# A last stage written anew: cosines spread by transfers, biases inside the turning products, all engines a batch apart

## The chip, the core and the metric

One core of a Trainium2 chip runs the whole kernel in one launch. PE (TensorE) multiplies matrices into PSUM, DVE (VectorE), ACT (ScalarE) and POOL (GpSimd) work on tiles of 128 partitions, SP issues most DMA transfers. Each engine takes its instructions in the order written; semaphores join them. The metric is the device time of an execution in microseconds (us).

## The reference, cut to what matters

A network of four layers runs on x of 8 x 512 x 128 floats; each adds `s * g` to x, where s is a sequence mixer and g a gate. The change lies in the last mixer, a state-space layer with rotated queries and keys (4 heads of 64, 128 states), on `u = layernorm(x)` seen as 8 batches of 512 tokens here:

```python
proj = u @ W_in                     # z 256, x 256, Bg 128, Cg 128, dt, A, trap 4 each, angles 32
theta = cumsum(angles * dt)         # per head, over the tokens
Bn, Cn = rmsnorm(Bg) * B_norm_w, rmsnorm(Cg) * C_norm_w
K = rope(Bn + B_bias, theta)        # x1*c - x2*s, x1*s + x2*c for the first 64 states, the rest as it is
Q = rope(Cn + C_bias, theta)
# chunks of 64 with a carried state in the reference; the kernel takes the equal form over all 512 tokens:
y = (Q K^T * decays * steps, lower triangle) @ x + D * x
s = (y * silu(z)) @ W_out;   x = x + s * silu(ffn)
```

## The kernel before, in words

`ssm_phase` (from L3364) is the last stage. It runs over 8 batches `i`, in each over 4 heads `h`, with data held as channels x tokens, 128 x 512 float32. PSUM has 8 banks of 512 columns: 0 to 2 for the products of queries and keys, 3 and 4 for projections and for spread cosines, 5 and 6 for the outputs, 7 for angles, gates and the result.

Per batch, PE projects keys and queries (`keys_and_queries`), the gates z, the means of the squares (`means`), the swapped projections (`turned`, with columns exchanged so that a rotation is a sum of two products), the angles and the tokens x (L3458). ACT makes gates (Silu), squares (L3550), roots as Ln and Exp (L3553, L3555), sine and cosine (L3558 to L3561), and the decays of a head (Exp, L3592 and L3594, seven instructions). A function set that ACT doesn't hold costs an ACT_TABLE_LOAD. DVE multiplies angles by steps (L3660), sums them over the tokens (scan, L3662), brings them into one turn (`one_turn`, five instructions, L3667 to L3678), and norms keys and queries (L3696, L3698).

Per head, cosine and sine rows (32 partitions) are spread to 128 partitions by matmuls with constant matrices (`spread`, L3473, four passes). ACT adds a head's bias to the normed keys and queries (L3569). DVE's `prepare` makes both products, each with one input in PSUM, then the smaller of two decays (`low`, L3728); POOL adds the products (L3613) to kq; PE multiplies keys by queries (L3484, eight passes); DVE's `weigh` multiplies by the decays (L3739, L3742, seven instructions), which POOL has multiplied by step factors on the diagonal blocks (L3637); PE multiplies by the tokens (L3496):

```python
v.scalar_tensor_tensor(out=t2[:, h % 2, n, :], in0=ps[:, 3, :], scalar=1.0, in1=tb[:, n, :],
                       op0=ALU.add, op1=ALU.mult)
last = v.scalar_tensor_tensor(out=t3[:, h % 2, n, :], in0=rot[:, n, :],
                              scalar=W("bc_rb")[:, n * H + h:n * H + h + 1], in1=ps[:, 4, :],
                              op0=ALU.add, op1=ALU.mult)
```

The order is written out by hand on each engine. PE: spread(0), the skipped part D x, spread(1), product(0), spread(2), product(1), spread(3), product(2), outputs of heads 0 and 1, angles of the next batch, product(3), the next batch's projections and means, outputs of heads 2 and 3, `turned`. POOL's step factors (`steps`, L3623 and L3629, three instructions a head) for all four heads stand at the start of the batch. SP (from L3385) sends the steps `dtb` (four transfers to 32 partitions, L3398), the summed decays `ellb` (four, to 128 partitions, L3403) and stores the result two batches later. After the last head DVE gates the outputs (L3761), PE projects them, DVE multiplies by the block's gate and adds (L3685, L3687).

Of the kernel before, what the change touches and what calls it, by code (L numbers as in the profile page):

```python
# [12 lines left out]
ALU = mybir.AluOpType  # L13
# [5 lines left out]
NB = T // 128  # L19
# [3344 lines left out]
def ssm_phase(nc, K, out_to):  # L3364
# [6 lines left out]
    Q_, K_ = 0, 1  # L3371
    with Stage(nc, K, at_once=True) as ctx:
        S = sems(nc, ctx, "ss", "dx bcps ang pj2 xt sq ms std rs norm at th n n1 c1 c2 clamp "
                 "sin abs cos cosm turn yz sps s gx sum stored z0 z0sb z1 z1sb")
        R = sems(nc, ctx, "ssr", "dt", 2)
        HD = sems(nc, ctx, "sh", "ell cps b0 t2 turned qk low dec m1 m2 dm a y", H)
# [3 lines left out]
        sq, xt, th = sb("sq", 2, T), sb("xt", NB, 256), sb("th", 3, T)  # L3380
        dtb, ellb, low = sb("dtb", 2, T), sb("ellb", H, T), sb("low", 2, NB, 128)
        tb, t2, t3 = sb("tb", 2, T), sb("t2", 2, 2, T), sb("t3", 2, 2, T)
        kq, dec = sb("kq", 2, 2, T), sb("dec", H, SPAN)
        mm, own = sb("mm", H, NB, 128), sb("own", NB, 128)
        y, table = sb("y", 2, T), sb("table", B)  # L3385
        block = stage_block(nc, K, ctx)

        @block.sync
        def _(sp):
            def store(i):  # L3390
                sp.wait_ge(S["sum"], i + 1)
                sp.dma_start(out_to[:, i * T:(i + 1) * T], X[:, i * T:(i + 1) * T]).then_inc(S["stored"], 16)

            for i in range(B):
# [5 lines left out]
                for h in range(H):  # L3400
                    sp.wait_ge(HD["dec"][h], i)
                    sp.wait_ge(HD["low"][h], i)
                    sp.dma_start(ellb[:, h, :], Rd[1, i * H + h:i * H + h + 1, :].to_broadcast([128, T])  # L3403
                                 ).then_inc(HD["ell"][h], 16)
                if i >= 2:
                    store(i - 2)
            store(B - 2)
            store(B - 1)
            sp.wait_ge(S["stored"], 16 * B)

        @block.tensor
        def _(pe):
            def project(i, bank, w):
                return pe.matmul(ps[:, bank, :], w, XN[:, i * T:(i + 1) * T], start=True, stop=True)  # L3414


            def keys_and_queries(i):
                pe.wait_ge(HD["t2"][H - 1], i)
# [3 lines left out]
            def means(i):  # L3422
                pe.wait_ge(HD["a"][H - 1], i)
                pe.wait_ge(S["sq"], i + 1)
                for n in range(2):
                    last = pe.matmul(ps[:, n, :], cst("mean"), sq[:, n, :], start=True, stop=True)  # L3426
                last.then_inc(S["ms"], 1)

            def turned(i):
                pe.wait_ge(S["std"], i + 1)  # L3430
                project(i, 0, W("in_turned")[:, 0:128])
                project(i, 1, W("in_turned")[:, 128:256]).then_inc(S["turn"], 1)

            def angles(i):
                if i >= 2:
                    pe.wait_ge(S["s"], i - 1)
                project(i, 7, W("in")[:, 768:896]).then_inc(S["ang"], 1)

            def gates(i):
                pe.wait_ge(S["at"], i + 1)  # L3440
                project(i, 7, W("in")[:, 0:128]).then_inc(S["z0"], 1)
                pe.wait_ge(S["z0sb"], i + 1)
                project(i, 7, W("in")[:, 128:256]).then_inc(S["z1"], 1)

            def out(i):

                pe.wait_ge(S["yz"], i + 1)
                pe.wait_ge(S["z1sb"], min(i + 2, B))
# [5 lines left out]
            def turn(i):  # L3454
                pe.wait_ge(S["yz"], i)
                pe.wait_ge(S["z1sb"], i + 1)
# [4 lines left out]
                last.then_inc(S["pj2"], 1)  # L3461
                if i:
                    out(i - 1)
                pe.wait_ge(S["norm"], i + 1)
                pe.wait_ge(S["cosm"], i + 1)
                pe.wait_ge(S["sin"], i + 1)

                def spread(h):

                    if h:  # L3470
                        pe.wait_ge(HD["t2"][h - 1], i + 1)
                    for n in range(2):
                        last = pe.matmul(ps[:, 3 + n, :], cst(("spread", "spread_sin")[n])[:, h * 128:(h + 1) * 128],  # L3473
                                         th[:, 1 + n, :],
                                         start=True, stop=True)
                    last.then_inc(HD["cps"][h], 1)

                def products(h):
                    pe.wait_ge(HD["turned"][h], i + 1)
                    if h:  # L3480
                        pe.wait_ge(HD["a"][h - 1], i + 1)
                    for jk in range(NB):
                        at, n = KEYS_AT[jk], T - 128 * jk
                        last = pe.matmul(ps[:, at // T, at % T:at % T + n], kq[:, h % 2, K_, jk * 128:(jk + 1) * 128],  # L3484
                                         kq[:, h % 2, Q_, jk * 128:T], start=True, stop=True)
                    last.then_inc(HD["qk"][h], 1)

                def outputs(pair):

                    for h in pair:  # L3490
                        pe.wait_ge(HD["a"][h], i + 1)
                    for jk in range(NB):
                        at, n = KEYS_AT[jk], T - 128 * jk
                        for h in pair:
                            r = slice(64 * (h % 2), 64 * (h % 2) + 64)
                            last = pe.matmul(ps[r, 5 + h // 2, jk * 128:T], xt[:, jk, h * 64:(h + 1) * 64],  # L3496
                                             dec[:, h, at:at + n], start=False,
                                             stop=(jk == NB - 1), skip_group_check=True)
                            if jk == NB - 1:
                                last.then_inc(HD["y"][h], 1)  # L3500

                spread(0)

                pe.wait_ge(S["xt"], i + 1)
                for n in range(2):
                    pe.matmul(ps[:, 5 + n, :], dx[:, n * 128:(n + 1) * 128], XN[:, i * T:(i + 1) * T],
                              start=True, stop=False, skip_group_check=True)
                spread(1)
                products(0)
# [5 lines left out]
                if i + 1 < B:  # L3515
                    angles(i + 1)
# [562 lines left out]
```

## Time and profile before

| | |
|---|---|
| median of 3 runs | 2919.72 us (2915.32 to 2923.3) |
| profiled execution, its own time | 2923.67 us |
| its span | 2921.9 us |
| PE, DVE, ACT, POOL busy in the span | 81%, 74%, 59%, 35% |
| mean granted clock of TensorE | 0.891 |
| the stage changed | 2579 to 2921.9 us |

Times in the trace are from the start of the span. The span leaves out a little of what the device time counts, here 1.8 us. The shares are means over stages with different limits, so the stage is read alone. In it PE issues a float32 matmul as two passes, each with a weight load.

### The profile page before, as it was taken

How to read it: one execution, taken by the hardware profiler on the slowest of the kernel's cores; microseconds unless marked ns; L12 is line 12 of the kernel's file. 1: busy time of each engine (PE TensorE's matmuls, PEld its weight loads, DVE VectorE, ACT ScalarE, POOL GpSimd, SP SyncE). 2: the span in 40 equal slices, each digit the busy share in tenths (PEclk: the TensorE clock that was granted, in tenths of full speed). 3: DMA queues.
4: the chain of work that ended last, by engine and by line, in shares of the span. 5: the costliest groups of instructions: out<-in, count | busy, mean ns of one | idle time of the engine just before them, and what ended most of it. 6: DMA issues, size and time to landing. Idle time of an engine off the chain costs nothing. (4 is left out here: it accounts for less than half of the span.)

```text
span 2921.9 us, 36852 instructions
## 1 busy us (share of the span) xinstructions
PE 2356.4 (81%) x10377; PEld 1044.9 (36%) x10472; DVE 2165.8 (74%) x5969; ACT 1709.4 (59%) x3093; POOL 1015.9 (35%) x979
## 2 busy tenths in 40 slices
PE   7666378786778999769999989778788888768887
PEld 2211267663343434333333333323331111234443
DVE  6999589995686665456666666587579999567777
ACT  4444344543656666462222278646579999677775
POOL 0222489992244555240000044200020000048886
PEclk8777566776889999889999999989889999889999
DMA  3112575625175765431111033100031111011110
GB/s 131 58 58 72 136 133 109 107 41 147 52 227 109 145 117 112 101 141 47 34 36 37 23 82 101 50 0 0 17 108 45 45 40 44 16 42 33 39 37 26
DMA packets 301385, 211.63 MB, mean 72 GB/s; under 512 B 157640, under 2 KB 266104, under 8 KB 300536
## 3 DMA queue, kind: packets, MB, share of 16 engines
q1 hardware_dynamic: 263216, 191.81, 24.5%
q0 software_dynamic: 19712, 14.96, 3.8%
q10 hardware_dynamic: 18256, 2.52, 0.5%
q8 instruction: 85, 1.39, 0.2%
q14 instruction: 116, 0.95, 0.1%
HBM read 136.18 MB, written 62.52 MB: 68 GB/s over the span
## 5 line engine op out<-in xcount | busy, mean ns | idle before, releaser
L3169 ACT ACTIVATE ca_pw<-ca_ps,ca_mx 128x512 f32<-128x512 f32 x512 | 342.7, 931 | 7.3 <-DVE ca_mx L3205 7.3
L3205 DVE TENSOR_REDUCE ca_mx<-ca_ps 128x1 f32<-128x512 f32 x512 | 311.2, 674 | 1.0 <-PE ca_ps L3136 1.0
L3002 DVE CUSTOM_DVE_ANT_0 mx_sums<-mx_ps,w_w2f 128x384 f32<-128x384 f32 (+3 forms) x512 | 218.1, 486 | 112.2 <-PE mx_ps L2957 110.7
L2945 PE MATMUL gm_ps<-gm_h,w_w2f 128*128 128x512 f32 x512 | 239.0, 607 | 3.1 <-DVE gm_h L3030 3.1
L3169 ACT ACTIVATION_READ_ACCUMULATOR ca_pw<-ca_ps,ca_mx 128x1 f32 x512 | 230.6, 450 | 0.0
L3136 PE MATMUL ca_ps<-qs,ks 128*128 128x512 bf16 x484 | 173.6, 399 | 59.2 <-ACT ca_pw L3169 39.5
L2644 ACT ACTIVATE ta_pw<-ta_ps,w_cst 128x1280 f32<-128x1280 f32 x128 | 168.0, 1322 | 35.8 <-PE ta_ps L2524 35.7
L3074 ACT ACTIVATE gm_h<-gm_ps,w_w2f 128x512 f32<-128x512 f32 x64 | 44.0, 687 | 218.4 <-PE gm_ps L2945 218.4
L2370 ACT ACTIVATE at_pw<-at_ps 128x1280 f32<-128x1280 f32 x128 | 157.1, 1238 | 23.7 <-PE at_ps L2337 23.6
L2776 DVE TENSOR_TENSOR ta_pw<-ta_pw,w_cst 128x384 f32<-128x384 f32 x128 | 70.7, 552 | 130.8 <-ACT ta_pw L2644 127.0
L2689 POOL DMA_INDIRECT Acc<-XN,f_idx x64 | 104.4, 1631 | 152.4 <-DVE XN L2747 137.8
L3146 PE MATMUL ca_o<-ca_pw,ca_vs 128*32 128x512 f32 x1024 | 138.4, 616 | 2.5 <-POOL ca_vs L3180 2.5
L2384 POOL MEMSET at_qs<- 128x1024 uint32 x4 | 3.7, 952 | 379.2 <-POOLq L2854 379.2
L3180 POOL TENSOR_TENSOR ca_vs<-VA,ca_rz 128x64 f32<-128x64 f32 x64 | 19.0, 297 | 329.3 <-DVE ca_rz L3192 329.3
L3136 PEld LDWEIGHTS ca_ps<-qs,ks 128*128 128x128 bf16 x512 | 40.2, 96 | 259.8 <-ACT ca_pw L3169 225.2
L724 DVE TENSOR_REDUCE rs_st<-rs_run 128x32 f32<-128x128 f32 x512 | 122.0, 284 | 13.4 <-ACT XN L749 13.2
L2945 PEld LDWEIGHTS gm_ps<-gm_h,w_w2f 128*128 128x128 f32 x512 | 91.3, 189 | 106.8 <-issue 101.5
L2401 DVE TENSOR_TENSOR at_pw<-at_pw,w_cb_f 128x384 f32<-128x384 f32 x128 | 70.4, 555 | 59.5 <-ACT at_pw L2370 59.5
L622 PE MATMUL ex_hps<-ex_xgt,ex_w 128*128 128x128 f32 x384 | 68.5, 333 | 48.1 <-ACT ex_h L778 25.3
L707 DVE TENSOR_TENSOR rs_run<-rs_st,rs_lay 128x96 f32<-128x96 f32 x512 | 105.6, 248 | 0.1
L2393 POOL TENSOR_SCALAR_AFFINE_SELECT at_pw<-at_pw 128x128 f32<-128x128 f32 x128 | 73.5, 575 | 91.0 <-ACT at_pw L2370 91.0
L2351 PE MATMUL at_o<-at_pw,at_va 128*32 128x256 f32 (+2 forms) x1280 | 95.8, 392 | 8.4 <-DVE at_pw L2401 5.9
(573 smaller groups left out, 6183.9 us busy)
## 6 DMA issues: line engine op xcount, KB each, us to landing
Pd<-s_p SPq DMA_DIRECT2D x48, 384.0 KB, 4.5
ex_w<-e_w SPq DMA_DIRECT2D x48, 256.0 KB
Qd<-rp_q SPq DMA_DIRECT2D x4, 2048.0 KB, 9.6
ss_ellb<-Rd SPq DMA_DIRECT2D x32, 256.0 KB, 3.3
qs<-Pd SPq DMA_DIRECT2D x32, 192.0 KB, 4.1
ks<-Pd SPq DMA_DIRECT2D x32, 192.0 KB, 4.2
Pd<-cs_p SPq DMA_DIRECT2D x16, 384.0 KB, 2.4
GX<-Qd SPq DMA_DIRECT2D x44, 128.0 KB
```

What stands on the lines that cost most here:

```text
L707: v.tensor_tensor(rows(n, 0, 3, half)[:, :, :, :, 0], state(n - 1, half).unsqueeze(1).to_broadcast([128, 3, V4, N]), given(n, KK, 3), ALU. ...
L724: v.tensor_reduce(state(n, half).rearrange("p v k -> p (v k)"), rows(n, 2, 2, half).rearrange("p r v k s -> p (v k) r s"), AX.XY, ALU.add) ...
L2351: last = pe.matmul(O[32 * a:32 * a + 32, G % 2, t0:t1], va[:, jk, G % GROUPS * GH + a].rearrange("p d x -> p (d x)"), pw[:, (GH * G + a) % ...
L2370: act.activation(pw[:, s % BUF, 0:SPAN], ps[:, s % 2, 0:SPAN], ACT.Exp, scale=float(1 / np.sqrt(D))).then_inc(S["power"], 1)
L2644: act.activation(pw[:, s % BUF, 0:SPAN], ps[:, s % 2, 0:SPAN], ACT.Square, scale=0.25 * 0.5 ** 0.5, bias=cst("rhalf")).then_inc(S["power"], 1)
L2689: g.indirect_dma_start(Acc, bass.IndirectOffsetOnAxis(ap=idx[:, u // 2, at:at + 1], axis=0), y[:, u % 2, c, :], None, compute_op=ALU.add). ...
L2945: last = pe.matmul(at, W(("h1", "h2")[layer])[:, j * 512 + f * 128:j * 512 + (f + 1) * 128], (h0, h1)[layer][:, j, :], start=(j == 0), sto ...
L3002: return v.tensor_tensor_reduce(out=sums[:, bank, at:at + n], in0=ps[:, bank, at:at + n], in1=K["w2f"]("down")[:, T - n:T], scale=-1.0, sc ...
L3136: pe.matmul(ps[:, q % BANKS, :], ks[:, G % 2, h % GH, jk * 128:(jk + 1) * 128], qs[:, G % 2, h % GH, :], start=True, stop=True).then_inc(S ...
L3146: last = pe.matmul(O[32 * a:32 * a + M, G % 2, :], vs[:, h % BUF, jk, :], pw[:, h % BUF, jk, :], start=(jk == 0), stop=(jk == NB - 1), ski ...
L3169: act.activation(pw[:, h % BUF, jk, :], ps[:, (h * NB + jk) % BANKS, :], ACT.Exp, bias=mx[:, h % H, jk:jk + 1], accum_out=z[:, h % H, jk:j ...
L3205: v.tensor_reduce(mx[:, h % H, jk:jk + 1], ps[:, q % BANKS, :], AX.X, ALU.max, negate=True).then_inc(S["top"], 1)
```

## The change

`ssm_phase` is rewritten; the arithmetic is the same.

- **Cosines.** `spread` and its constants go. ACT writes three rows of results, cosine, sine and minus sine, to `trig`. SP copies them for each head from SBUF to SBUF into `cs`, in two transfers: to partitions 0 to 31 cosine and minus sine, to 32 to 63 cosine and sine. Partitions 64 to 127 hold 1 and 0, set once. `cs` has two places (h even, odd); `trig` has one, and ACT waits with the next batch's until all four heads' copies have landed.
- **Biases.** ACT's biased copies go. DVE adds the head's bias inside both products, and both now have two inputs in SBUF; the first is written to kq itself, POOL adds the second to it.
- **Order.** Each engine's order spans two batches: DVE prepares head 0 of batch i+1 before it weighs head 3 of batch i, POOL makes step factors a batch ahead between the heads, ACT makes the next batch's sines at the start of a batch and its roots at the end. The two means share bank 7 one after the other, the two gates are one ACT instruction over banks 3 and 4.

The core of the diff (steps, `weigh`, `lowest`, `finish`, `store` and the angles keep their instructions):

```diff
+            def turns_of(i, h):
+                sp.wait_ge(S["cos"], i + 1)
+                if h >= 2:
+                    sp.wait_ge(HD["t2"][h - 2], i + 1)
+                else:
+                    sp.wait_ge(HD["t2"][h + 2], i)
+                at = slice(32 * h, 32 * h + 32)
+                sp.dma_start(cs[0:32, h % 2], trig[at, COS:DOWN + 1]).then_inc(HD["cs"][h], 16)
+                sp.dma_start(cs[32:64, h % 2], trig[at, COS:UP + 1:UP]).then_inc(HD["cs"][h], 16)
...
+            for i in range(B):
+                turns_of(i, 2)
+                if i + 2 < B:
+                    steps_of(i + 2)
+                if i + 1 < B:
+                    sums_of(i + 1, 0)
+                    sums_of(i + 1, 1)
+                turns_of(i, 3)
+                if i + 1 < B:
+                    turns_of(i + 1, 0)
+                    sums_of(i + 1, 2)
+                    sums_of(i + 1, 3)
+                    turns_of(i + 1, 1)
+                if i:
+                    store(i - 1)
...
+            def means(i, n):
+                if n:
+                    pe.wait_ge(S["ln0"], i + 1)
+                else:
+                    pe.wait_ge(S["sq"], i + 1)
+                    pe.wait_ge(S["at"], max(i + 1, 2))
...
+            for i in range(B):
+                products(i, 0)
+                if i:
+                    outputs(i - 1, (2, 3))
+                    if i + 1 < B:
+                        keys_and_queries(i + 1)
+                products(i, 1)
+                tokens(i)
+                if i + 1 < B:
+                    means(i + 1, 0)
+                products(i, 2)
+                if i + 1 < B:
+                    means(i + 1, 1)
+                skipped(i)
+                outputs(i, (0, 1))
                 if i:
                     out(i - 1)
...
+                products(i, 3)
                 if i + 1 < B:
                     turned(i + 1)
+                if i + 2 < B:
+                    angles(i + 2)
+                if i + 1 < B:
+                    gates(i + 1)
...
+            def turns(i):
+                act.wait_ge(S["clamp"], i + 1)
+                for h in range(H):
+                    act.wait_ge(HD["cs"][h], 32 * i)
+                act.activation(trig[:, UP, :], phase[:, i % 2, :], ACT.Sin)
+                act.activation(trig[:, DOWN, :], phase[:, i % 2, :], ACT.Sin, scale=-1.0)
+                act.activation(trig[:, COS, :], phase[:, i % 2, :], ACT.Abs).then_inc(S["abs"], 1)
+                act.wait_ge(S["abs"], i + 1)
+                act.activation(trig[:, COS, :], trig[:, COS, :], ACT.Sin, scale=-1.0, bias=cst("halfpi")).then_inc(S["cos"], 1)
...
+            for i in range(B):
+                if i:
+                    gates(i)
                 if i + 1 < B:
+                    turns(i + 1)
+                decays(i, 2)
+                if i + 1 < B:
+                    squares(i + 1)
+                decays(i, 3)
+                tokens(i)
+                if i + 1 < B:
+                    roots(i + 1)
+                    decays(i + 1, 0)
+                    decays(i + 1, 1)
...
+            for i in range(B):
+                more = i + 1 < B
+                turned(i, 1)
+                if more:
+                    steps(i + 1, 0)
+                turned(i, 2)
+                weighed(i, 2)
+                if more:
+                    steps(i + 1, 1)
+                turned(i, 3)
+                weighed(i, 3)
+                if more:
+                    steps(i + 1, 2)
+                    turned(i + 1, 0)
+                    weighed(i + 1, 0)
+                    steps(i + 1, 3)
+                    weighed(i + 1, 1)
...
+            def prepare(i, h):
+                v.wait_ge(HD["cs"][h], 32 * (i + 1))
+                v.wait_ge(S["bc"], i + 1)
+                v.wait_ge(S["rot"], i + 1)
+                for n, side_of in ((0, K_), (1, Q_)):
+                    v.scalar_tensor_tensor(out=kq[:, h % 2, side_of, :], in0=bc[:, n, :],
+                                           scalar=W("bc_b")[:, n * H + h:n * H + h + 1], in1=cs[:, h % 2, 0, :],
+                                           op0=ALU.add, op1=ALU.mult)
+                    last = v.scalar_tensor_tensor(out=side[:, h % 2, side_of, :], in0=rot[:, n, :],
+                                                  scalar=W("bc_rb")[:, n * H + h:n * H + h + 1], in1=cs[:, h % 2, 1, :],
+                                                  op0=ALU.add, op1=ALU.mult)
+                last.then_inc(HD["t2"][h], 1)
...
             for i in range(B):
+                more = i + 1 < B
+                prepare(i, 1)
+                lowest(i, 2)
+                weigh(i, 0)
+                if i:
+                    gated(i - 1)
+                prepare(i, 2)
+                lowest(i, 3)
+                weigh(i, 1)
+                prepare(i, 3)
+                weigh(i, 2)
+                if more:
+                    normed(i + 1)
                 if i:
                     finish(i - 1)
...
+                if more:
+                    turned(i + 1)
+                if i + 2 < B:
+                    add_angles(i + 2)
+                if more:
+                    lowest(i + 1, 0)
+                    lowest(i + 1, 1)
+                    prepare(i + 1, 0)
+                weigh(i, 3)
+                if i + 2 < B:
+                    one_turn(i + 2)
```

The loops over `i` are, in this order, SP's, PE's, ACT's, POOL's and DVE's.

## Rows read from the trace of the kernel before

**Rows 1.** Busy time by stretch: us; PE, PEld, DVE, ACT, POOL busy; PEclk, DMA share, GB/s

```profile
2740.80:2781.40 40.60, 35.19 (x117) 16.48 (x118) 31.96 (x64) 29.22 (x52) 33.05 (x37) 1.00 0.14 39
```

**Rows 2.** The chain that ended last, in time: start us, us, what

```profile
2602.17 0.67 DVE ss_t L3718
...
2819.49 2.42 PE ss_ps L3484 x8
...
2827.44 2.59 PE ss_ps L3414 x6
...
2841.66 1.97 PE ss_ps L3473 x4
...
2860.03 2.42 PE ss_ps L3484 x8
```

**Rows 3.** Waits of three batches, 2740.8 to 2862.5: us in total, times, longest

```profile
DVE ss_y L3761 <- PE ss_ps L3496: 10.9, 3, 3.6
```

**Rows 4.** DVE in order of time, first stage: start us, us, instruction

```profile
99.46 1.85 DVE L206 SCALAR_TENSOR_TENSOR rp_t<-SX,w_w 128x512 f32<-128x512 f32 x1
101.23 1.75 DVE L203 TENSOR_TENSOR GX<-GX,rp_t 128x512 f32<-128x512 f32 x1
```

**Rows 5.** POOL in the same stretch

```profile
99.50 1.26 POOL L233 TENSOR_TENSOR rp_t<-SX 128x512 f32<-128x512 f32 x1 [1.23 <-DVE SX L203]
100.72 1.71 POOL L235 TENSOR_TENSOR rp_t<-rp_ew,SX 128x512 f32<-128x512 f32 x1
```

**Rows 6.** POOL's lines in the stage: duration ns min/median/max, first and last start us

```profile
L3613 POOL TENSOR_TENSOR ss_kq<-ss_t x64: 1258/1274/1726, 2602.9 to 2904.8; 128x512 f32<-128x512 f32 x64
...
L3623 POOL TENSOR_TENSOR ss_own<-w_cst,COL x32: 1042/1049/1057, 2588.4 to 2884.6; 128x512 f32<-128x512 f32 x32
...
L3637 POOL TENSOR_TENSOR ss_dec<-ss_dec,ss_mm x128: 445/458/1392, 2606.7 to 2907.3; 128x128 f32<-128x128 f32 x128
```

**Rows 7.** DVE's groups by form from 2579 us: busy us, mean ns, idle before

```profile
L3718 DVE SCALAR_TENSOR_TENSOR ss_t<-ss_rot,w_w3a,ss_ps 128x512 f32<-128x512 f32 x64 | 47.2, 737 | 0.0
...
L3662 DVE TENSOR_TENSOR_SCAN ss_th<-w_cst,ss_th 128x512 f32<-128x512 f32 x8 | 10.0, 1248 | 0.3
...
L3702 DVE TENSOR_SCALAR ss_th<-ss_th 128x512 f32<-128x512 f32 x8 | 7.6, 948 | 0.5 <-ACT ss_th L3561 0.5
L3672 DVE SCALAR_TENSOR_TENSOR ss_th<-ss_th 128x512 f32<-128x512 f32 x8 | 5.5, 693 | 0.3
...
L3670 DVE TENSOR_SCALAR ss_th<-ss_th 128x512 f32<-128x512 f32 x8 | 3.4, 427 | 0.3
```

**Rows 8.** ACT in order of time, one batch

```profile
2791.94 1.28 ACT L3553 ACT_TABLE_LOAD   x1
...
2798.03 0.63 ACT L3558 ACTIVATE ss_th<-ss_th 128x512 f32<-128x512 f32 x1
...
2807.05 0.39 ACT L3592 ACTIVATE ss_dec<-ss_low,COL 128x128 f32<-128x128 f32 x1
...
2809.12 0.39 ACT L3592 ACTIVATE ss_dec<-ss_low,COL 128x128 f32<-128x128 f32 x1
```

**Rows 9.** The steps' tile: issues ns min/median/max, their reader, landing us

```profile
L3398 SPq DMA_DIRECT2D ss_dtb<-Rd x32: 303/422/2006, 2579.0 to 2827.0; - x32
L3660 DVE TENSOR_TENSOR ss_th<-ss_ps,ss_dtb x8: 691/692/692, 2582.5 to 2865.9; 128x512 f32<-128x512 f32 x8
...
DMA to landing us min/median/max: 1.8/2.8/3.7
```

**Rows 10.** DVE in order of time: the first of a weigh and what follows it

```profile
2816.99 0.28 DVE L3739 TENSOR_TENSOR ss_dec<-ss_ps,ss_dec 128x128 f32<-128x128 f32 x1
...
2818.96 0.68 DVE L3716 SCALAR_TENSOR_TENSOR ss_t<-ss_ps,ss_tb 128x512 f32<-128x512 f32 x1
```

**Rows 11.** Busy time by stretch at the stage's start, columns as in rows 1

```profile
2586.00:2596.40 10.40, 6.17 (x18) 2.88 (x16) 5.07 (x8) 9.98 (x12) 8.77 (x9) 1.00 0.06 21
2596.40:2599.80 3.40, 3.25 (x4) 1.50 (x5) 0.05 (x1) 2.49 (x4) 3.32 (x4) 0.50 0.02 5
```

More of the change, by code:

```diff
@@ L3434, in angles @@
[L3434 to L3448, printed above, removed]
-                for n in range(2):
-                    last = pe.matmul(ps[:, 7, :], W("out")[:, n * C:(n + 1) * C], y[:, n, :],
-                                     start=(n == 0), stop=(n == 1))
-                last.then_inc(S["sps"], 1)
@@ new lines, in out @@
+            def out(i):
+                pe.wait_ge(S["yz"], i + 1)
+                if i + 2 < B:
+                    pe.wait_ge(S["ln1"], i + 3)
+                else:
+                    pe.wait_ge(S["s"], i)
+                for n in range(2):
+                    last = pe.matmul(ps[:, 7, :], W("out")[:, n * C:(n + 1) * C], y[:, n, :],
+                                     start=(n == 0), stop=(n == 1))
+                last.then_inc(S["sps"], 1)
+            pe.wait_ge(S["dx"], 1)
+            angles(0)
@@ new lines, in _ @@
+            gates(0)
+            keys_and_queries(0)
+            angles(1)
+            means(0, 0)
+            means(0, 1)
+            turned(0)
+            keys_and_queries(1)
+            for i in range(B):
[13 more added lines that the diff above has]
+                outputs(i, (0, 1))
@@ L3462, in turn @@
                 if i:
                     out(i - 1)
[L3464 to L3509, printed above, removed]
-                spread(2)
-                products(1)
-                spread(3)
-                products(2)
-                outputs((0, 1))
-                if i + 1 < B:
-                    angles(i + 1)
@@ L3517, in turn @@
-                products(3)
-                if i + 1 < B:
-                    keys_and_queries(i + 1)
-                    gates(i + 1)
-                    means(i + 1)
-                outputs((2, 3))
+                products(i, 3)
                 if i + 1 < B:
                     turned(i + 1)
-            pe.wait_ge(S["dx"], 1)
-            angles(0)
-            keys_and_queries(0)
-            gates(0)
-            means(0)
-            turned(0)
-            for i in range(B):
-                turn(i)
+                if i + 2 < B:
+                    angles(i + 2)
@@ L3597, in turn, with decays @@
-                if i + 1 < B:
-                    gates_and_roots(i + 1)
-            gates_and_roots(0)
-            for i in range(B):
-                turn(i)
+            def decays(i, h):
+                act.wait_ge(HD["ell"][h], 16 * (i + 1))
+                act.wait_ge(HD["low"][h], i + 1)
+                act.wait_ge(HD["y"][h], i)
+                for jk in range(NB):
+                    at, n = KEYS_AT[jk], T - 128 * jk
+                    fall = COL[:, 3, jk, i * H + h:i * H + h + 1]
+                    last = act.activation(dec[:, h, at:at + 128], low[:, h % 2, jk, :], ACT.Exp, bias=fall)
+                    if n > 128:
+                        act.activation(dec[:, h, at + 128:at + n], ellb[:, h, (jk + 1) * 128:T], ACT.Exp, bias=fall)
+                last.then_inc(HD["dec"][h], 1)
@@ new lines, in _ @@
+            gates(0)
+            squares(0)
+            turns(0)
+            roots(0)
+            decays(0, 0)
+            decays(0, 1)
+            for i in range(B):
+                if i:
+                    gates(i)
+                if i + 1 < B:
+                    turns(i + 1)
[8 more added lines that the diff above has]
+                    decays(i + 1, 1)
```

348 lines of the change are left out of this document (172 added, 176 removed).

## The prediction

> **What bounds the kernel now.** The change touches the last stage alone, 2579 to 2921.9 us. I read its stretches of one batch first: PE is busy 35.2 of 40.6 us, POOL 33, DVE 32, ACT 29, at the full granted clock [rows 1]. No engine is full, so the chain says who sets the pace. It repeats every 40.54 us (a product of queries and keys starts at 2819.49 and its like at 2860.03) [rows 2]: spread cosines on PE, turn on DVE, add on POOL, product on PE, weigh on DVE, head after head, then projections, roots, the next batch's norms. The reader should see that DVE waits 3.6 us a batch for the last outputs before it can gate them [rows 3], and all that follows is behind that. The change attacks this latency.
>
> **What moves the other way.** See one DVE instruction with both inputs in SBUF beside POOL [rows 4, 5]. POOL's add of 99.50 ends at 100.76, the DVE instruction issued at 99.46 ends at 101.31, POOL's next, issued at 100.72, at 102.43, and DVE's, issued at 101.23, at 102.98. They take turns: 0.55 us for the DVE one after POOL's end (alone 0.69), 1.12 for POOL's (alone 1.26). So each holds something for its duration less 0.14 us, and the other does not run. In this stage POOL's short multiply, 0.458 us at the median, takes 1.392 when the scan is in its way [rows 6], and the one-input subtract takes 0.95 where its like with POOL idle takes 0.43 [rows 7]. An instruction with one input in PSUM stays at 0.74 whatever POOL does [rows 7]. Today's turning reads one input from PSUM; the new one reads both from SBUF, 16 times a batch.
> The Trainium skill (SBUF — State Buffer, "Who interferes with whom") has the rule: a DVE instruction with two SBUF inputs, or in a two-port mode, and a GpSimd instruction that reads SBUF exclude each other for the whole instruction. The trace agrees with the exclusion, but the hold is 0.14 us shorter than the instruction.
>
> **The change part by part, one batch in the middle.**
> PE loses 16 spread passes at 0.43 us (6 passes take 2.59 [rows 2]), 6.9 us. The wait for cosines in PSUM goes. What is late next is below.
> ACT loses 8 biased copies (5.3 us by 0.67 each) and the 0.2 us table filler, gains a third sine (0.54) and splits one Ln; table loads stay five at 1.28 [rows 8]. About 24 of 29 us remain: no bound, but its order matters.
> DVE: 16 turning instructions at 0.69 (both inputs in SBUF, as the row of L3672 [rows 7]) for 16 at 0.68 to 0.74, minus the 0.95 subtract: some 1.7 us less, 30.2 us if never held up.
> POOL keeps every instruction. Held time: 8 adds x 1.13, 8 step multiplies x 0.91, 4 step adds x 1.13 (1.27 alone, like the adds of heads), 16 multiplies x 0.32 = 26.0 us (each duration of [rows 6] less 0.14).
> DVE's claims on the same thing: before, 4 "low" and 3 others x 0.55, the scan 1.11, 4 one-input x 0.29 = 6.1; after, 16 x 0.55 more and one subtract less = 14.6 us. So the shared demand goes from 32.1 to **40.6 us a batch**. That alone equals today's period: whatever the pipeline hides, the period can't go below 40.6.
> SP gets 8 issues a batch more, 0.42 us each. Their landing isn't in the trace; the nearest transfer to 32 partitions lands in 1.8 to 3.7, median 2.8 [rows 9]. They move twice its bytes, so I take 3.0 for the second of a pair, after 0.85 of issue and 0.1 of wait: 4.0 us from release to cosines in place; 2.7 to 5 are its ends.
> The prologue: two batches' angles on DVE, gates before keys on PE. Worked forward: first angles from 2582.5, when the steps have landed [rows 9], brought into one turn by 2587.4; the second batch's product with the steps, for which the first mean must wait, 2588.1; sines to 2589.9 and, with two table loads, both Ln, the second mean and Exp, to 2595.8; norms on DVE 2597.1, turned projections on PE 2599.1, turned norms 2600.4, first head prepared 2602.9. Before, that is at 2602.8 [rows 2]. Nothing gained.
>
> **Walk of the period.** Let T be the end of prepare(i,1). It releases the transfer of head 3's cosines, and ACT's new angles (one buffer) wait for that landing. ACT: landed T+4.0; four functions 2.45; the Exp load 1.3; decays of head 2 2.5 [rows 8]; squares 0.95; decays of head 3 2.5; tokens 0.95; Ln load 1.3 and Ln 0.6: T+16.6. PE may then compute the second mean (1.1), and behind it in its queue stand skipped (1.7), outputs (2.3), out (1.7), the product of head 3 (2.2), turned (1.9): T+27.5. DVE: turned 1.5, angles with the scan 2.0, two "low" 1.3, prepare(i+1,0) 2.5: T+34.8, call it E. POOL has had nothing since T+27 but waits for E.
> From E on both engines have work: weigh(i,3) takes 2.0 [rows 10] while POOL adds 2.5. Then DVE's five angle instructions meet POOL's four short multiplies (ends E+5.8, not 4.8), and prepare(i+1,1)'s four meet three step instructions and one multiply: 4 x 0.56 + 0.91 + 0.91 + 1.13 + 0.33 = 5.6 instead of 2.5. T' = E+11.4. Period 34.8 + 11.4 = **46.2 us**.
> Cross-check: between T and T+16 DVE has 13.3 us of work plus some 4 of taking turns: it waits for ACT and PE, not they for it. The shared thing is idle 5.6 of 46.2 us, mostly before E.
> The end: after the last prepare(7,0) no further batch covers anything. Head by head, add 2.5, product 2.2, weigh 2.0, three times, then outputs, gate, out, sum, store: 38.7 us; before 35.1 (2921.9 - 2602.8 - 7 x 40.57).
> Span: 2602.9 + 7 x 46.2 - 2.0 (the first period has no weigh of a batch before) + 38.7 = 2963. That is 41 over the profiled span 2921.9. The profiled run itself was 2923.7, 4.0 above the median of 2919.7, so the median becomes **2961**.
> With the skill's rule taken literally (whole durations) the sum would be 30.8 + 18.4 = 49.2 a batch, the span 2984.
>
> **Rivals.** A comparison can tell about 0.3% (9 us) from nothing.
> *The pipeline hides it, faster.* The mechanism: DVE keeps its present 8.6 us of waits a batch, now over 30.2 us of work, since its new instructions fall where POOL is idle or slip beside it. Period 38.8, end 36: 2602.9 + 271.6 - 2 + 36 = 2908, median 2906. For: POOL idles before E, PE and ACT each lose work. Against: it needs the shared demand of 40.6 to be wrong by 2 us and my chain by 7. It decides where the period is under 40.6. 13%.
> *The shared demand is met without gaps.* Period 40.6: 2602.9 + 284.2 - 2 + 38.7 = 2924, median 2922, no change. For: cosines landing early and an ACT that never waits would let POOL run on. Against: POOL can't add head 0 before E. 12%. It also holds the case in which the change pipelines less than it says (one buffer of cosines ties batch i+1 to head 3 of batch i) and so keeps today's rhythm.
> *TensorE's clock falls.* PE's true work drops to 26 of 46 us with two gaps of 6 us each. At 2596.4 to 2599.8, after 10.4 us in which PE was busy 6.2, the granted clock is 0.50 (1.2 of 2.4 GHz) and four spread passes take that whole stretch, 3.25 us, against 1.97 at full [rows 2, 11]. The gaps sit before work with slack, but PE's 11 us run on the chain may start at half: 3.5 us a batch, period 49.7, span 2987, median 2985. Ends 0 and 10 us a batch. 17%.
> *Holds for whole durations.* A mechanism in which a two-input DVE instruction and a POOL one never overlap at all, recorded start to recorded end: period 49.2 or more, median 2982. Against it stand the 0.55 and 1.12 of [rows 4, 5]. 4%. This is what the page of the Trainium skill named above (SBUF — State Buffer, "Who interferes with whom") says to the letter.
>
> **How the numbers follow.** My forecast has 54%, around it landings of 2.7 to 5 us and a looser or tighter meeting at E: period 43.5 to 49, 2942 to 2981. With the floor below and the clock above, the range is 2920 to 2992; beyond it lie most of the faster case and the ends of the clock's. Faster by over 0.3%: 0.14; within: 0.11; slower: 0.75.
>
> **What would show it.** Right: the period at 44 to 49 us; DVE's turning at a mean near 1.0 to 1.3 us, not 0.69; POOL's adds over 1.4; DVE waiting for PE's turned projections and POOL idle just before; ACT waiting for cosines to land. Wrong: turning at 0.69 beside a busy POOL, or a period under 40.6. The clock rival shows as a granted clock well under 1.00 in the middle stretches and products at twice 2.4 us.

## The result, and the profile after

The changed kernel takes 2965.94 us, the median of 4 runs (2964.92 to 2966.89). The kernel before, on the same chip, takes 2920.39. The ratio is 1.0154 [1.0143, 1.0166]: slower by 1.5%, 4.9 us above the forecast of 2961 and inside its range. The profiled execution has a span of 2963.2 us, with a mean granted clock of 0.876; the forecast of the span was 2963. That it fits to the microsecond is luck: the parts below are off by 7 to 15 us, with both signs. The 4.9 us come from the step from span to median: the forecast took off 4.0 us because the profiled execution of the kernel before was that much above its median, and that of the changed kernel (2964.92 us) is its fastest.

The stretches of the changed kernel; columns: us; busy time (and instructions) of PE, PEld, DVE, ACT and POOL; granted clock, DMA share, GB/s.

```profile
0.00:2579.00 2579.00, 2067.16 (x9466) 910.81 (x9561) 1910.11 (x5465) 1475.38 (x2678) 751.24 (x692) 0.88 0.32 77
2579.00:2963.00 384.00, 263.49 (x784) 127.90 (x784) 313.50 (x498) 184.79 (x345) 294.77 (x288) 0.85 0.20 55
2677.60:2722.40 44.80, 32.31 (x100) 16.14 (x99) 38.82 (x63) 23.00 (x43) 37.05 (x37) 0.85 0.23 58
2722.40:2767.30 44.90, 32.01 (x100) 15.79 (x99) 38.98 (x64) 22.99 (x43) 37.17 (x38) 0.85 0.22 60
```

The stage starts at the same time as before. A batch has gone from 40.6 to 44.9 us. Against [rows 1], PE and ACT are less busy (32.0 for 35.2, 23.0 for 29.2), as the change means them to be. DVE and POOL are busier (39.0 for 32.0, 37.2 for 33.1), although DVE has lost an instruction. The granted clock has fallen from 1.00 to 0.85.

Its costliest groups from 2579 us on; columns: count, then busy us, mean ns of one, then idle time before it and what ended it.

```profile
L3676 POOL TENSOR_TENSOR ss_dec<-ss_dec,ss_mm 128x128 f32<-128x128 f32 x128 | 86.4, 705 | 0.0
L3667 POOL TENSOR_TENSOR ss_kq<-ss_kq,ss_side 128x512 f32<-128x512 f32 x64 | 84.8, 1346 | 69.8 <-DVE ss_side L3751 69.8
L3751 DVE SCALAR_TENSOR_TENSOR ss_side<-ss_rot,w_w3a,ss_cs 128x512 f32<-128x512 f32 x64 | 71.6, 1119 | 0.0
L3748 DVE SCALAR_TENSOR_TENSOR ss_kq<-ss_bc,w_w3a,ss_cs 128x512 f32<-128x512 f32 x64 | 69.4, 1084 | 0.1
```

The turning products take 1.08 and 1.12 us in the mean. With one input in PSUM they took 0.74 [rows 7]. POOL's short multiply stands at a mean of 0.705. In the kernel before its median is 0.458 [rows 6], but its mean, with which 0.705 has to be compared, is 0.564:

```profile
L3637 POOL TENSOR_TENSOR ss_dec<-ss_dec,ss_mm 128x128 f32<-128x128 f32 x128 | 68.0, 564 | 14.3 <-ACT ss_dec L3592 13.7
```

DVE and POOL side by side; columns: start us, us, then engine, line, operation, names, shapes and count.

```profile
2736.66 0.74 DVE L3748 SCALAR_TENSOR_TENSOR ss_kq<-ss_bc,w_w3a,ss_cs 128x512 f32<-128x512 f32 x1
...
2744.83 1.23 POOL L3656 TENSOR_TENSOR ss_mm<-w_cst,COL 128x512 f32<-128x512 f32 x1
2745.07 1.53 DVE L3748 SCALAR_TENSOR_TENSOR ss_kq<-ss_bc,w_w3a,ss_cs 128x512 f32<-128x512 f32 x1
...
2746.02 1.49 POOL L3656 TENSOR_TENSOR ss_own<-w_cst,COL 128x512 f32<-128x512 f32 x1
...
2746.53 1.53 DVE L3751 SCALAR_TENSOR_TENSOR ss_side<-ss_rot,w_w3a,ss_cs 128x512 f32<-128x512 f32 x1
...
2747.59 1.59 POOL L3662 TENSOR_TENSOR ss_mm<-ss_mm,ss_own 128x512 f32<-128x512 f32 x1
...
2747.99 1.75 DVE L3748 SCALAR_TENSOR_TENSOR ss_kq<-ss_bc,w_w3a,ss_cs 128x512 f32<-128x512 f32 x1
```

The first row is a product while POOL has nothing: 0.74 us (the forecast took 0.69). The others are the same instruction beside POOL's steps: DVE's end follows POOL's by 0.54 us (2746.06 to 2746.60), and POOL's next one ends 0.91 us after that (2747.51). That is the alternation of [rows 4, 5], now in the middle of every batch.

The waits in 2690 to 2880 us, some four batches; columns: total us, times, longest.

```profile
ACT ss_dec L3623 <- DVE ss_low L3762: 53.1, 5, 10.6
...
ACT ss_trig L3590 <- DMA ss_cs<-ss_trig: 39.2, 4, 9.8
POOL ss_kq L3667 <- DVE ss_side L3751: 36.6, 9, 6.8
...
DVE ss_bc L3732 <- ACT ss_sq L3608: 8.4, 4, 2.1
DVE ss_rot L3739 <- PE ss_ps L3451: 7.6, 4, 1.9
```

ACT waits 9.8 us a batch for head 3's cosines to land before it may write the next ones. POOL waits for the first turning of a batch, up to 6.8 us. The next rows are PE's and POOL's instructions at that point (timeline; in brackets the idle time before).

```profile
2739.47 2.49 POOL L3667 TENSOR_TENSOR ss_kq<-ss_kq,ss_side 128x512 f32<-128x512 f32 x2 [6.79 <-DVE ss_side L3751]
...
2742.01 4.21 PE L3513 MATMUL ss_ps<-ss_kq 128*128 128x512 f32 x8 [6.27 <-POOL ss_kq L3667]
...
2753.76 0.63 ACT L3590 ACTIVATE ss_trig<-ss_phase 128x512 f32<-128x512 f32 x1 [9.84 <-DMA ss_cs<-ss_trig]
```

After 6.3 us without work PE runs its product at about half clock (granted 0.57 from 2742.0 to 2746.2): 4.21 us, where [rows 2] have 2.42.

**The sum, by the marks of the prediction.** E is the end of a batch's first turning, `prepare(i,0)`, T that of `prepare(i,1)`, from the ends of the instructions of L3751:

| | before | forecast | after |
|---|---|---|---|
| E of batch 0 | 2602.8 | 2602.9 | 2610.3 |
| first period | | 44.2 | 39.4 |
| a middle period | 40.57 | 46.2 | 44.83 (four), 44.88 (one) |
| last period | | 46.2 | 42.98 |
| E to T, in the middle | | 11.4 | 11.21 |
| T to the next E | | 34.8 | 33.6 |
| seven periods | 284.0 | 321.4 | 306.6 |
| from the last E to the end | 35.1 | 38.7 | 46.3 |

Of the 41.3 us lost, 22.6 lie in the periods, 7.5 at the start and 11.2 in the tail.

### The profile page after: what moved, and what is told of

It reads as the page before. It is cut to its first block and busy times, and to the rows that moved or that the text cites. A ratio compares the mean times of both kernels' runs of the same rounds, so it can differ in the third digit from the quotient of the medians.

```text
span 2963.2 us, 36595 instructions
## 1 busy us (share of the span) xinstructions
PE 2330.6 (79%) x10249; PEld 1038.7 (35%) x10344; DVE 2223.6 (75%) x5963; ACT 1660.2 (56%) x3022; POOL 1046.0 (35%) x979
## 5 line engine op out<-in xcount | busy, mean ns | idle before, releaser
L3169 ACT ACTIVATION_READ_ACCUMULATOR ca_pw<-ca_ps,ca_mx 128x1 f32 x512 | 236.9, 463 | 0.0
L3513 PE MATMUL ss_ps<-ss_kq 128*128 128x512 f32 (+3 forms) x256 | 108.3, 583 | 83.4 <-POOL ss_kq L3667 82.9
L3513 PEld LDWEIGHTS ss_ps<-ss_kq 128*128 128x128 f32 x256 | 61.6, 251 | 146.0 <-POOL ss_kq L3667 100.6
L3667 POOL TENSOR_TENSOR ss_kq<-ss_kq,ss_side 128x512 f32<-128x512 f32 x64 | 84.8, 1346 | 69.8 <-DVE ss_side L3751 69.8
```

Of the source, the lines that this page charges most:

```text
L3169: act.activation(pw[:, h % BUF, jk, :], ps[:, (h * NB + jk) % BANKS, :], ACT.Exp, bias=mx[:, h % H, jk:jk + 1], accum_out=z[:, h % H, jk:j ...
L3667: last = g.tensor_tensor(kq[:, h % 2, n, :], kq[:, h % 2, n, :], side[:, h % 2, n, :], ALU.add)
```

## The experiments

Ratios are to the kernel before, run beside the one tested; its own median lay at 2918.76, 2931.97 and 2934.46 us in the three sets of runs, some 0.5% apart, so ratios are compared and not times. Periods are those of the middle batches.

**e1: the same pipeline, second input of the turning from PSUM.** The price of the shared resource is taken off DVE's products; instructions, waits and transfers stay.

```diff
-  scalar=W("bc_b")[...], in1=cs[:, h % 2, 0, :],
+  scalar=W("bc_b")[...], in1=ps[:, 4, :],
-  scalar=W("bc_rb")[...], in1=cs[:, h % 2, 1, :],
+  scalar=W("bc_rb")[...], in1=ps[:, 4, :],
```

Bank 4 is set to 1 once; the second projection of each pair goes to bank 3, which both readers read, so the result is not the reference's.

> The changed kernel, but each of the 16 turning instructions of a batch reads a constant from PSUM in place of the cosine row in SBUF (bank 4 is set to 1 once; the second projection of each pair goes to bank 3 as well, so queries, the second gate and the turned queries are not what the reference has; all transfers, waits and instruction counts stay). Theory 1 (turning and POOL exclude each other because both inputs are in SBUF): turning at 0.7 us each whatever POOL does, prepare(i,1) 2.7 us instead of 5.4, period 44.8 to 42.0 us, time 2940 us (2932 to 2948). Theory 2 (the ring through the cosines' transfers sets the period, the exclusion is absorbed): period 44.8, time 2966 us.

Measured: 2942.03 us against 2918.76, ratio 1.0073 [1.0054, 1.0091]. Period 42.0, E to T 8.4 us, tail 42.3. The groups from 2579 us, as above:

```profile
L3751 DVE SCALAR_TENSOR_TENSOR ss_side<-ss_rot,w_w3a,ss_ps 128x512 f32<-128x512 f32 x64 | 47.2, 737 | 0.0
L3748 DVE SCALAR_TENSOR_TENSOR ss_kq<-ss_bc,w_w3a,ss_ps 128x512 f32<-128x512 f32 x64 | 47.1, 736 | 0.1
...
L3676 POOL TENSOR_TENSOR ss_dec<-ss_dec,ss_mm 128x128 f32<-128x128 f32 x128 | 65.1, 538 | 2.2 <-ACT ss_dec L3623 2.2
```

With the second input's address changed, the product is back at 0.737 us and POOL's short multiply falls from 0.705 to 0.538. What E to T loses, 2.8 us, the period loses too; T to E stays at 33.6. Half of the slowdown is this. The other half isn't: this kernel is still slower than before.

**e2: two places for ACT's cosines.** The wait of 9.8 us goes.

```diff
-  trig = sb("trig", 3, T)
+  trig = sb("trig", 2, 3, T)
-  act.wait_ge(HD["cs"][h], 32 * i)
+  act.wait_ge(HD["cs"][h], 32 * (i - 1))
```

> The changed kernel with two places for the rows of cosines and sines, so that ACT's next angles do not wait for the landing of head 3's copies. Theory 1: ACT's wait of 9.8 us goes, but the decays of head 3 then wait for the low of head 3, which DVE gives only 9.8 us after prepare(i,1), held up by taking turns with POOL; gain 0.5 us a batch, time 2962 us (2956 to 2966). Theory 2 (the ring through the one buffer of cosines sets the period): 3 to 6 us a batch less, time 2925 to 2945 us.

Measured: ratio 1.0141 [1.0123, 1.0158], period 44.6. The wait is gone and yields 0.2 us a batch, where 0.5 were expected; the ratios alone don't tell this kernel from the changed one. Behind the wait stands another: ACT's decays of head 3 now wait 3.9 us a batch for DVE's `low` (15.7 us in four batches), which comes late because DVE and POOL take turns.

**e3: both edits.**

> Both edits of the two runs before together (output again not the reference's in queries, second gate and turned queries). Theory 1: with turning unhindered the low of head 3 comes 7.2 us after prepare(i,1), and without the wait for the landing ACT can use that; period about 39 us, time 2918 us (2908 to 2930). Theory 2: what the second run gives, and nothing more from the PSUM reads.

Measured: ratio 1.0022 [1.0011, 1.0033]. Period 40.0 to 40.7, E to T 8.4 us, tail 40.7. Alone the edits are worth 2.8 and 0.2 us a batch, together 4.5: two limits lie side by side, and each hides the other. The period was to be 39; it is some 1.3 higher, and what keeps it there wasn't taken apart. So the pipeline, with the price of the shared resource and of the single place gone, ends level with today's 40.57 a batch. Its first batch (E at 2610.9 in a span of 2926.4) and its tail of 40.7 are still longer than before's.

**e4: the kernel before, its products with both inputs in SBUF.** The counterpart of e1: the suspected cost is given to a kernel that hasn't got it. The rotation is not computed.

```diff
-  in0=ps[:, 3, :], scalar=1.0, in1=tb[:, n, :],
+  in0=bc[:, n, :], scalar=1.0, in1=tb[:, n, :],
-  scalar=W("bc_rb")[...], in1=ps[:, 4, :],
+  scalar=W("bc_rb")[...], in1=bc[:, n, :],
```

> The kernel before, with one thing of the change alone: its 16 turning instructions of a batch read both inputs from SBUF (bc in place of the spread cosines in PSUM, so the rotation is not computed; spreads, waits, biased copies and order stay). Theory 1 (exclusion): turning at a mean near 1.0 us, POOL's adds over 1.35, period 40.6 to about 44.5 us, time 2950 us (2935 to 2960). Theory 2 (both inputs in SBUF cost nothing, the rest of the rewrite does it): turning at 0.69, time 2918 us (2914 to 2922).

Measured: 2966.62 us, ratio 1.0161 [1.0142, 1.018], period 46.0 to 47.0. The groups from 2579 us:

```profile
L3637 POOL TENSOR_TENSOR ss_dec<-ss_dec,ss_mm 128x128 f32<-128x128 f32 x128 | 99.6, 806 | 15.5 <-ACT ss_dec L3592 15.5
L3613 POOL TENSOR_TENSOR ss_kq<-ss_t 128x512 f32<-128x512 f32 x64 | 87.9, 1393 | 10.9 <-DVE ss_t L3718 10.9
...
L3716 DVE SCALAR_TENSOR_TENSOR ss_t<-ss_bc,ss_tb 128x512 f32<-128x512 f32 x64 | 66.6, 1041 | 25.0 <-PE ss_ps L3473 25.0
L3718 DVE SCALAR_TENSOR_TENSOR ss_t<-ss_rot,w_w3a,ss_bc 128x512 f32<-128x512 f32 x64 | 60.8, 950 | 0.0
```

Two addresses cost the old kernel as much as the whole rewrite costs. The mechanism is shown; its size was missed: 5.5 to 6.5 us a batch where 4 were expected. A likely reason is that in the old order every turning stands between PE and PE, with nothing to absorb it; and POOL's short multiply, in the chain too, goes from 0.564 to 0.806.

**e5: POOL's first steps held back until the first angles are in one turn.** One line on POOL: `g.wait_ge(S["clamp"], 1)` ahead of its first `steps`.

> The changed kernel with one wait more: POOL's first step factors start only when batch 0's angles are brought into one turn, as in the kernel before. In the changed kernel they run beside the angles, and the five instructions of the first turn take 6.8 us (2584.3 to 2591.1) instead of 2.9. Theory 1 (exclusion also makes the start late): the first head is prepared 3.9 us earlier, at about 2606.4 instead of 2610.3, periods unchanged at 44.8, time 2962 us (2959 to 2964). Rival (the start is late for the halved clock and the transfers): 2966 us, first head at 2610.

Measured: 2976.84 us against 2931.97, ratio 1.0145 [1.0128, 1.0162]. The interval holds the 1.0154 of the changed kernel, so the total decides nothing. The timelines of the start do. The changed kernel, then e5:

```profile
2578.39 0.42 DVE L3794 TENSOR_TENSOR ss_dx<-w_w3a 128x256 f32<-128x256 f32 x1 [1.43 <-PEq L3221]
...
2584.33 1.09 DVE L3716 TENSOR_SCALAR ss_step<-ss_phase 128x512 f32<-128x512 f32 x1
...
2586.86 1.42 DVE L3720 SCALAR_TENSOR_TENSOR ss_phase<-ss_step,ss_phase 128x512 f32<-128x512 f32 x1
...
2589.76 1.37 DVE L3726 TENSOR_SCALAR ss_phase<-ss_phase 128x512 f32<-128x512 f32 x1
```

```profile
2593.03 0.43 DVE L3795 TENSOR_TENSOR ss_dx<-w_w3a 128x256 f32<-128x256 f32 x1 [1.44 <-PEq L3221]
...
2598.51 0.43 DVE L3717 TENSOR_SCALAR ss_step<-ss_phase 128x512 f32<-128x512 f32 x1
...
2599.43 0.69 DVE L3721 SCALAR_TENSOR_TENSOR ss_phase<-ss_step,ss_phase 128x512 f32<-128x512 f32 x1
...
2600.88 0.43 DVE L3727 TENSOR_SCALAR ss_phase<-ss_phase 128x512 f32<-128x512 f32 x1
```

The five instructions of a turn take 6.8 us beside POOL's steps and 2.8 alone. From the first row of each, batch 0's angles are ready after 12.7 us there and 8.3 here. Yet E of batch 0 comes after 31.9 and 30.9 us: the same steps now run beside the second batch's angles, whose five instructions take 6.8 us in their turn. Of 4.4 us gained 1.0 arrives, where 3.9 were expected.

**e6: PE given filler work**, so that its clock stays up: the gates' projections are issued four times, the keys' and queries' three times, from the second or third batch on.

> The changed kernel with TensorE's two gaps of a batch filled: the gate projections are issued four times and the key and query projections three times, the last one counting. Theory 1 (the clock costs nothing on the chain, since the products that run at half clock are waited for by nobody): granted clock 0.98 to 1.00 in the middle stretches instead of 0.85, products 2.2 us instead of 4.2 to 4.6, but period 44.8 as before, time 2964 us (2960 to 2968). The clock rival: 2 to 3.5 us a batch back, 2942 to 2952 us.

Measured: ratio 1.0157 [1.014, 1.0174]. Four batches of it:

```profile
2690.00:2870.00 180.00, 153.31 (x476) 73.37 (x474) 155.02 (x249) 91.98 (x172) 148.43 (x146) 0.96 0.22 59
```

The clock goes from 0.85 to 0.96 and the period stays at 44.85 (one of the five middle ones takes 45.35). The low clock costs the middle batches nothing. Nor does the filler hide a gain by standing in the way: the turned projections, for which DVE waits, run at a granted clock of 1.00 in both kernels, 2.74 us for six passes, and DVE waits 1.9 us a batch for them in both (2.4 in the odd one of e6). PE's slow products end before POOL and DVE have come round.

**e7: the step multiplications on ACT**, which has time: eight of POOL's 12 wide instructions a batch become ACT's, with the step as their scale; POOL keeps the sums, in a slightly different order.

```diff
-  last = g.tensor_tensor(mm[:, h] if n == 0 else own[:], cst(src)..., COL[...]..., ALU.mult)
+  last = act.activation(to[:, j, :], cst(src), ACT.Identity, scale=COL[:, c, j, i * H + h:i * H + h + 1])
```

> The changed kernel with the step factors' multiplications moved from POOL (8 a batch, 0.91 us of hold each) to ACT (32 of 128 columns, 0.3 us each, in ACT's idle 10 us), POOL keeps their sums. Theory 1: the shared demand falls from 40.6 to 33.3 us a batch; from prepare(i+1,0) to prepare(i+1,1) 9.4 us instead of 11.2, the rest of the ring unchanged (33.6), period 43.0; the start 4 us earlier and the end 3 us shorter; time 2948 us (2940 to 2955). Rival (the turning is slow for another reason than POOL): 2966 us or, if ACT's added 9.6 us stand in the ring, more.

Measured: ratio 1.0115 [1.0098, 1.0132], expected 1.0095. Period 43.7 to 43.9, but 45.4 once, expected 43.0; E to T 10.0 us, expected 9.4. DVE's products, the same groups as above, still stand at 0.87 to 0.98 us in the mean, so POOL's sums and decays, which stay, are in their way too. Some of the demand taken away probably lay where DVE had nothing to turn; that wasn't measured.

```profile
L3756 DVE SCALAR_TENSOR_TENSOR ss_kq<-ss_bc,w_w3a,ss_cs 128x512 f32<-128x512 f32 x64 | 62.5, 976 | 0.1
L3759 DVE SCALAR_TENSOR_TENSOR ss_side<-ss_rot,w_w3a,ss_cs 128x512 f32<-128x512 f32 x64 | 55.5, 868 | 0.0
```

**e8: e7 and e2 together.**

> The same with two places for the rows of cosines as well. Theory 1: now the low of head 3 sets when ACT can make its decays, and with less taking of turns it comes 8.5 instead of 9.8 us after prepare(i,1); period 41.3, time 2935 us (2925 to 2943), 0.5% above the kernel before. Rival (the two waits add nothing to each other): as in the run before.

Measured: ratio 1.008 [1.0063, 1.0097], period 41.5 to 42.9. As in e3, the second place is worth more (1 to 2 us) once the shared demand is lower.

**e9: another order on PE**, so that nothing that must wait stands ahead of the next batch's turned projections: `products(i,3)`, `out(i-1)` and `turned(i+1)` first, `skipped` and `outputs(i,(0,1))` behind them; the end of the last batch is adapted.

> The changed kernel with TensorE's order alone changed: after the second mean come the product of head 3, the result of the batch before and the turned projections, and only then the skipped part and the outputs of heads 0 and 1 (4 us of matmuls fewer in the ring); at the very end the last result but one moves behind head 3. Theory 1: the product of head 3 then waits for POOL's add of head 3, which ends at 2727.2 where PE is free at 2722.4, so of the 4 us most is lost to that wait; period 44.0 to 44.8, time 2958 us on the chip of the first result, ratio to the kernel before 1.010 to 1.015. Rival (PE's queue alone makes the ring): 4 us a batch, ratio 1.004 to 1.006.

Measured: 2996.0 us against 2934.46, ratio 1.0204 [1.0187, 1.0221], period 47.2 to 47.7. Slower than the changed kernel by 2.3 to 2.9 us a batch, where a small gain was expected. The waits in 2650 to 2840 us, and PE's timeline:

```profile
ACT ss_dec L3626 <- PE ss_ps L3524: 55.7, 4, 14.4
```

```profile
2745.65 4.22 PE L3513 MATMUL ss_ps<-ss_kq 128*128 128x512 f32 x8 [4.80 <-POOL ss_kq L3670]
...
2751.42 2.74 PE L3451 MATMUL ss_ps<-XN,w_w3a 128*128 128x512 f32 x6
```

The product of head 3 is now PE's next instruction, waits 4.8 us for POOL's sum and then runs at about half clock (granted 0.56). So the turned projections (L3451) start 10.6 us after the second mean, which ends at 2740.84; in the changed kernel it is 7.9 us (2722.45 to 2730.37). These 2.7 us are what a period has lost. The next batch's decays need the places that the outputs of this one still read, and those outputs come later: ACT waits up to 14.4 us a batch for them. Whether that adds anything wasn't separated. In the changed kernel's order PE computes skipped parts and outputs while POOL gets there. The queue that looked like an obstacle was a filler.

**e10: the edits of e8 and e9 at once**, with the decays' lows of heads 2 and 3 together and the last batches' end reordered.

> All that the runs before point to, with the reference's result: two places for the cosines, the step factors' multiplications on ACT, PE's order of the run beside this one, and DVE's low of head 3 ahead of its first weighing. With POOL's add of head 3 done early, PE's new order counts: the turned projections come 3.3 us earlier, ACT's decays of head 3 1 to 2 us earlier. Theory 1: period 41.5 to 37.5, the end 2 us shorter, ratio to the kernel before 0.995 to 1.002. Rival (another wait steps in, DVE's own 30 us and what is left of the taking of turns): period 39.5 or more, ratio over 1.003.

Measured: 2946.82 us, ratio 1.0040 [1.0026, 1.0055]; period 40.5 to 41.7, expected 37.5. The rival named there came true. Three quarters of the loss come back, but it doesn't beat the kernel before. Waits in 2640 to 2800 us:

```profile
PE ss_ps L3513 <- POOL ss_kq L3679: 38.2, 12, 5.7
POOL ss_kq L3679 <- DVE ss_side L3763: 34.9, 10, 7.8
```

PE waits for POOL and POOL for DVE: head after head the sum must still pass from one to the other. Which of these waits sets the period wasn't taken apart. No version ran that is faster than the kernel before.

## Why the prediction was right

**The cause** held. The forecast's claim was that a second SBUF input makes DVE and POOL take turns, and that this costs more than the removed latency. e1 takes the second input away (period 44.8 to 42.0), e4 gives it to the old kernel (40.6 to 46.0 or more). The means, 1.08 to 1.12 us, lie in the stated 1.0 to 1.3. It isn't the whole cause: without it the rewritten stage still needs 42.0 us a batch, and 40.0 to 40.7 only when the one place for cosines is gone too (e3). One named sign failed: POOL's adds were to be over 1.4 us and stand at a mean of 1.346, no longer than in the kernel before (1.374). The price falls on DVE's products and on POOL's short multiplies.

**The shared demand**, by the forecast's estimate 40.6 us a batch, is a floor that no period of the changed kernel crossed, save the first, 39.4, in which less work is claimed. The actual 44.83 stands 4.2 above, for times in which neither engine claims the resource. A part of them lies in POOL's wait of 6.8 us just before E; DVE's scan, two `low` and first four products fill the rest of that wait.

**The walk.** E to T was 11.4 and is 11.21; T to E was 34.8 and is 33.6. The term over-sized is the landing: I took 4.0 us from release to cosines in place. T at 2750.60 and ACT's start at 2753.76 make 3.2. The transfers of `cs`:

```profile
L3417 SPq DMA_DIRECT2D ss_cs<-ss_trig x32: 532/538/562, 2593.6 to 2922.7; - x32
L3418 SPq DMA_DIRECT2D ss_cs<-ss_trig x32: 632/633/662, 2594.2 to 2923.3; - x32
...
DMA to landing us min/median/max: 2.2/2.3/3.7
```

A landing takes 2.3 us, not the 3.0 from the nearest transfer [rows 9]; the issue costs SP 0.54 and 0.63 us, more than the 0.42 I had put. That explains 0.8 of the 1.4 us by which a period is shorter. And the walk followed one limit only. e2 shows another 0.2 us behind it: had the landing cost nothing, the period would have been 44.6 all the same, by a way through the alternation that I hadn't walked.

The larger miss lies in the two periods at the ends. Of the 14.8 us that the seven periods were put too long, 6.8 lie in the five middle ones, 4.8 in the first and 3.2 in the last. For the first I took off a `weigh`, 2.0 us, and so had 9.4 us from E to T; but no angles are brought into one turn there either, and none of POOL's steps run beside it: 4.86 us. In the last no angles are left to sum: 31.8 us from T to E.

**The start, "Nothing gained"**, is the first step that failed: 7.4 us were lost. I had worked the angles forward with durations of DVE alone, and forgot that POOL's first twelve step instructions run there from 2579 to 2595. The alternation of [rows 4, 5] was known; it wasn't applied to the prologue. Against the marks of the forecast 3.7 us are lost when the first angles are in one turn (2591.1 for 2587.4), 5.1 when the norms start (2600.9 for 2595.8) and 6.9 when the turned norms start (2606.0 for 2599.1). e5 shows 4.4 us of the alternation on the first angles, of which only 1.0 reaches E, since it moves on to the second batch's. In e7 POOL's step multiplications are gone from the start altogether, and E comes 3.1 us sooner. A part of the rest is PE's clock, which the forecast had at full: the second mean takes 2.08 us at a granted clock of 0.50, where a middle batch has 1.13, and the turned projections 3.62 at 0.54, where four passes took 1.97 [rows 2]. How much of the remaining 4.3 us that is stays open.

**The tail, 38.7**, is the second: 46.3. The sum was a chain of durations, each head add, product, weigh. As printed it doesn't even give 38.7: three rounds of 6.7 are 20.1, and from the last weighing to the end of the span are 11.3 us, together 31.4; only a fourth round, that of head 0, brings it near (38.1). The timeline of the last batch has a queue in it:

```profile
2917.00 2.49 POOL L3667 TENSOR_TENSOR ss_kq<-ss_kq,ss_side 128x512 f32<-128x512 f32 x2 [4.95 <-DVE ss_side L3751]
2919.45 3.49 POOL L3676 TENSOR_TENSOR ss_dec<-ss_dec,ss_mm 128x128 f32<-128x128 f32 x4
2922.90 1.49 POOL L3656 TENSOR_TENSOR ss_mm<-w_cst,COL 128x512 f32<-128x512 f32 x1
2924.36 1.04 POOL L3656 TENSOR_TENSOR ss_own<-w_cst,COL 128x512 f32<-128x512 f32 x1
2925.48 1.27 POOL L3662 TENSOR_TENSOR ss_mm<-ss_mm,ss_own 128x512 f32<-128x512 f32 x1
2926.70 2.60 POOL L3676 TENSOR_TENSOR ss_dec<-ss_dec,ss_mm 128x128 f32<-128x128 f32 x4
2929.26 6.27 POOL L3667 TENSOR_TENSOR ss_kq<-ss_kq,ss_side 128x512 f32<-128x512 f32 x4
```

```profile
2919.54 4.12 PE L3513 MATMUL ss_ps<-ss_kq 128*128 128x512 f32 x8 [4.43 <-POOL ss_kq L3667]
2923.59 2.38 PE L3524 MATMUL ss_ps<-ss_dec,ss_xt 128*64 128x512 f32 x16
2932.68 4.44 PE L3513 MATMUL ss_ps<-ss_kq 128*128 128x512 f32 x8 [6.72 <-POOL ss_kq L3667]
```

Head 1's turning is done at 2922.6, but its sum stands behind two sets of decays and the steps of head 3 and starts at 2929.26. From product(7,0) to product(7,1) are 13.1 us; my chain gave add, product and weigh, 6.7. The difference of 6.4 is most of the 7.6, and a part of it is the clock: the second product takes 4.44 us instead of 2.4.

So 7.4 and 7.6 too little, 14.8 too much: a total that fits because the terms cancel. That is luck; the cause and the middle period, 46.2 for 44.83, are what the forecast had right.

**The rivals.** *The pipeline hides it* fell: no period at 38.8. *The demand met without gaps* fell too; e3 has its period, 40.0 to 40.7, but with 8.8 us less of demand (16 x 0.55), so it doesn't show that case. *TensorE's clock falls*: it did fall, to 0.85, as named, and it costs nothing in the middle (e6), where its lower bound of 0 was the value; at the start and in the tail slow instructions do stand on the chain (2.08 for 1.13, 4.44 for 2.4). *Holds for whole durations*, 49.2 us a batch, is excluded by 44.83. The Trainium skill (SBUF — State Buffer, "Who interferes with whom") is right on who excludes whom, e1 and e4 agree; the length it states, the whole instruction, is more than these traces show: POOL's end comes 0.91 us after DVE's (2746.60 to 2747.51) for an instruction of 1.05.

## What to carry to other kernels

Before moving an operand from PSUM to SBUF, see what runs on POOL beside the instruction that reads it: the same DVE product took 0.74 us one way and 1.1 the other, and in the old kernel the price (1.6%) was as large as that of the whole rewrite. Add up what both engines claim of the shared resource in a period, and in the prologue and the last batch by itself, as these have their own neighbours. A wait that is long (9.8 us here) isn't thereby worth its length: take it away together with the limit behind it, or the second will give back what the first had cost.

## What was not expected of the hardware

Changing two input addresses in the old kernel, 16 instructions a batch, cost 1.6%, as much as the whole rewrite; the same resource costs 2.8 us a batch in an order with slack and 5.5 or more in one without. A granted clock of TensorE of 0.85 instead of 0.96 left the period where it was (44.83 and 44.85; one middle period of e6 took 45.35). And 32 more ACT instructions a batch, each reading a constant matrix with a scale per partition, relieved POOL at less than they gave: in e7 E of batch 0 came 3.1 us earlier from the stage's start, and the ratio fell from 1.0154 to 1.0115. Whether they have a price of their own wasn't measured.
